# Reordering the hand-over from a network's first layer to its second in a two-layer scan-and-experts kernel

## Time and profile before

| | us |
|---|---|
| median of three runs | 1706.99 |
| lowest and highest run | 1702.88, 1707.31 |
| the profiled execution | 1704.18 |
| its span, first to last instruction | 1702.4 |
| PE busy | 1401.7 (82%) |
| DVE busy | 1130.0 (66%) |
| ACT busy | 736.2 (43%) |
| POOL busy | 570.4 (34%) |

### The profile page before, as it was taken

One profiled execution on the slowest core, in us unless ns is written; L12 is line 12 of the kernel. 1 busy time (PEld: TensorE's weight loads), 2 busy tenths in 40 slices (PEclk: granted clock), 3 DMA queues, 4 the chain that ended last, 5 costly groups with the idle time before them and its releaser, 6 DMA issues.

```text
span 1702.4 us, 23957 instructions
## 1 busy us (share of the span) xinstructions
PE 1401.7 (82%) x8273; PEld 857.9 (50%) x8273; DVE 1130.0 (66%) x2014; ACT 736.2 (43%) x1296; POOL 570.4 (34%) x442
## 2 busy tenths in 40 slices
PE   0156665788887468988979999999999999999998
PEld 0033333344444145655645566666666666666664
DVE  8999967898989546667665555555555555555332
ACT  3465562344444243333214544444444444444332
POOL 1243320132332243132113344344444444444333
PEclk9987776999999778988989999999999999999999
DMA  3434352433332364333126766766676666666454
GB/s 97 150 105 128 106 196 62 141 118 102 123 106 87 133 192 156 136 93 131 45 80 171 189 175 180 181 168 173 180 180 172 172 177 181 178 167 162 89 90 63
DMA packets 91060, 235.58 MB, mean 138 GB/s; under 512 B 13568, under 2 KB 13696, under 8 KB 90944
## 3 DMA queue, kind: packets, MB, share of 16 engines
q1 hardware_dynamic: 56592, 146.20, 25.4%
q0 software_dynamic: 34352, 87.84, 25.0%
HBM read 167.87 MB, written 66.13 MB: 137 GB/s over the span
## 4 chain that ended last, share of the span: by engine, by line
PE 60%; DVE 28%; issue 4%; DMA 3%; ACT 3%; POOL 1%; SPq 0%; POOLq 0%; DVEq 0%; ACTq 0%
PE psG L1442 32%; PE psO L1471 19%; DVE wkFD L1026 6%; PE psH L1451 3%; PE psX L1401 3%; DMA ST<-W 3%; DVE wkFD L1004 2%; DVE wkFN L997 2%; DVE wkFD L993 2%; DVE wkEU L1017 1%; DVE wkFD L1014 1%; DVE wkFN L1033 1%; DVE wkFN L1007 1%; DVE HS L1268 1%; DVE H L1260 1%
## 5 line engine op out<-in xcount | busy, mean ns | idle before, releaser
L1442 PE MATMUL psG<-Whi,XSp 128*128 128x352 f16 (+2 forms) x3000 | 671.2, 329 | 1.7 <-POOL Wlo L715 1.1
L1471 PE MATMUL psO<-Whi,HS 128*128 128x512 f16 (+1 forms) x1180 | 407.5, 398 | 0.0
L1442 PEld LDWEIGHTS psG<-Whi,XSp 128*128 128x128 f16 x3000 | 299.0, 100 | 181.8 <-issue 17.4
L1442 PE MATMUL psG<-Wlo,XSp 128*128 128x352 f16 (+2 forms) x1500 | 388.5, 329 | 0.0
L754 POOL DMA_INDIRECT out<-OB,posb x128 | 201.5, 1574 | 441.9 <-ACT OB L932 441.9
L1236 DVE SCALAR_TENSOR_TENSOR Wlo<-ST,Whi 128x1088 f16<-128x1088 f32 (+1 forms) x122 | 157.2, 1289 | 234.0 <-ACT Whi L892 233.9
L1471 PE MATMUL psO<-Wlo,HS 128*128 128x512 f16 (+1 forms) x590 | 235.6, 399 | 0.0
L912 ACT ACTIVATE H<-psG 128x352 f32<-128x352 f32 (+1 forms) x215 | 95.5, 444 | 259.9 <-PE psG L1442 259.7
L1260 DVE SCALAR_TENSOR_TENSOR H<-H,psG 128x352 f32<-128x352 f32 (+1 forms) x215 | 105.5, 491 | 145.0 <-ACT H L912 144.7
L1442 PEld LDWEIGHTS psG<-Wlo,XSp 128*128 128x128 f16 x1500 | 149.6, 100 | 93.1 <-issue 7.5
L1471 PEld LDWEIGHTS psO<-Whi,HS 128*128 128x128 f16 x1180 | 120.2, 102 | 125.3 <-issue 20.0
(11 more groups left out here) (185 smaller groups left out, 1566.3 us busy)
## 6 DMA issues: line engine op xcount, KB each, us to landing
ST<-W SPq DMA_DIRECT2D x136, 544.0 KB, 4.6
ST<-W SPq DMA_DIRECT2D x27, 512.0 KB, 4.2
slots<-OB SPq DMA_DIRECT2D x39, 256.0 KB, 2.0
wkK<-fT SPq DMA_DIRECT2D x32, 256.0 KB, 3.3
xrows<-XR SPq DMA_DIRECT2D x22, 256.0 KB, 3.7
OB<-x SPq DMA_DIRECT2D x16, 256.0 KB, 3.7
y0rows<-OB SPq DMA_DIRECT2D x16, 256.0 KB, 2.2
out<-OB SPq DMA_DIRECT2D x16, 256.0 KB, 2.1
```

What stands on the lines that cost most here:

```text
L1442: op = M.matmul(o, hx[:, x, q * P:q * P + P], w(half_, off + c, nn), start=first, stop=last)
L1471: op = M.matmul(psO[bank(o)][:, :], HS[a][:, x, q * P:q * P + P], columns[n](half_, off0 + q * 512, 512), start=(q == 0 and x == 0 and hal ...
```

## The change: what it does, and the diff

It has seven parts.

1. `gate_step(i)` is `i + 5`. Steps run to 15 only. What steps 16 to 18 did, and the routing, is now a list written by hand: gates and squares of tiles 11 to 15 first, then turns, logits and shared blocks 9 to 12 between one another.
2. In every odd step from 5 on another piece of weights is split, with a load before and after. Piece 19 is done at the end of step 15 (before: piece 14).
3. Turned tiles 11, 13 and 15 use PSUM bank `psX`, the other tiles of layer 0 `psG[0][1]`; odd tiles use a second buffer for `HT32`; the split forms of tiles 14 and 15 lie in `RT[1]`.
4. The one-hot rows of layer 0 are four wide instructions for 8 rows of 128 (`hot0`), and two for all 32 rows of 39 (in `places0`), where there were 8 times five (`hots`).
5. The counts come with `r_pos` 3, in the same PSUM bank; the copy of positions (`r_posb`) stands apart from `r_wts`.
6. Halves of layer-1 units stand wherever `(j + 5) * 4 // 5` steps up: from j = -3 to 35, one iteration in five without (j = 1, 6, 11, ... 31), and none after 35.
7. `after_half`, which issues the exponentials of the next unit, runs in all iterations.

```diff
 def gate_step(i):
-    return min(i + 5, 17)
+    return i + 5
...
-    for s in range(19):
+    for s in range(16):
...
+        yield from loads(2, 27)
+        if s >= 5 and s % 2 == 1:
+            yield from splits(1)
             yield from loads(2, 27)
-        if s < 3 or s >= 15:
-            yield from splits(2 if s >= 15 else 1)
-        elif s >= 4:
+        if s < 3:
+            yield from splits(1)
+        elif 4 <= s < 15:
             yield from splits(1, low=False)
...
+    def piece():
+        yield from loads(2, 27)
+        yield from splits(1)
+        yield from loads(2, 27)
...
+    yield "f_scale", 10
+    yield "x_load", 15
+    yield "k_turn", 15
+    yield from tiles(("f_tanh",), 14, 15)
+    yield from tiles(("gate", "f_sq"), 11)
+    yield "row", 10
+    yield "gu_pe", 9
+    yield "f_turn", 10
+    yield from tiles(("gate", "f_sq"), 12, 13)
+    yield "f_var", 11
+    yield from tiles(("gate", "f_sq"), 14, 15)
+    yield from tiles(("f_var",), 12, 13)
+    yield "f_scale", 11
+    yield "row", 11
+    yield from tiles(("f_lo", "logit"), 10)
+    yield "f_turn", 11
+    yield from tiles(("f_var",), 14, 15)
+    yield "gu", 9
...
+    yield from tiles(("f_lo", "logit"), 12)
+    yield "f_turn", 14
+    yield from piece()
+    yield from tiles(("f_lo", "logit"), 13)
+    yield "f_turn", 15
+    yield "gu", 10
...
+    yield "gu_pe", 11
+    yield "r_pos", 3
+    yield "r_posb", 3
+    yield from piece()
+    yield "places0", 0
+    for h in range(4):
+        yield "hot0", h
+    yield "h_turn", 10
+    yield "down", 9
     yield "gu_pe", 12
-    yield "r_pos", 3
-    yield "r_wts", 3
-    yield from loads(2, 27)
+    for h in range(4):
+        yield "hot0_pe", h
     yield "table0", 0
     for j in range(3):
         yield "gather", R0 + j
+    yield "gu", 11
+    yield "x2_load", 10
+    yield from piece()
+    yield "r_wts", 3
     for j in range(-4, NB0 + 2):
...
-        if j >= -2 and ((j + 2) * 32 // 42 != (j + 1) * 32 // 42 or j >= 39):
+        if (j + 5) * 4 // 5 != (j + 4) * 4 // 5 or j >= 38:
             yield from next_half()
         if n < S1:
             yield "gu", n
-        if n > R0 - 2:
-            yield from after_half()
+        yield from after_half()
...
-        f_bank = [psG[0][1], psX]
+        def f_bank(f):
+            return psX if f >= NT or f in (11, 13, 15) else psG[0][1]
...
+                after(V.tensor_tensor(B0, bc(iota16[:, 0:NB0].unsqueeze(1), [P, 32, NB0]),
+                                      bc(gj[:, ks].unsqueeze(2), [P, 32, NB0]), ALU.is_equal))
+                b = B0.rearrange("p (i k) n -> p i k n", k=2)
+                after(V.tensor_tensor(b, b, bc(tid.unsqueeze(2).unsqueeze(3), [P, 16, 2, NB0]), ALU.mult))
+
+            def hot0(h):
+                V.tensor_tensor(A0[:, 8 * h:8 * h + 8, :], bc(iota16[:, :].unsqueeze(1), [P, 8, P]),
+                                bc(qa[:, 8 * h:8 * h + 8].unsqueeze(2), [P, 8, P]), ALU.is_equal).then_inc(r_hot, 1)
...
             def f_turn(f):
...
-                if f >= 1:
+                if f == 11:
+                    eng.wait_ge(k_rt, KX)
+                elif 12 <= f < NT:
+                    eng.wait_ge(f_lo, f - 1)
+                elif f >= 1:
                     eng.wait_ge(f_lo, f)
```

More of the change, by code:

```diff
@@ L230, in stages @@
             yield "f_var", i
-        if s < 16:
+        if s < 15:
             yield "k_out", s
@@ L246, in stages, with tiles @@
             yield "dummies", 0
+    def piece():
+        yield from loads(2, 27)
+        yield from splits(1)
+        yield from loads(2, 27)
+    def tiles(what, *which):
+        for i in which:
+            for w in what:
+                yield w, i
+    yield "f_scale", 10
[16 more added lines that the diff above has]
+    yield "gu", 9
+    yield "x2_load", 8
+    yield "h_turn", 8
+    yield from tiles(("f_lo", "logit"), 11)
+    yield from tiles(("f_scale", "row"), 12, 13)
+    yield "down", 7
+    yield from tiles(("f_turn",), 12, 13)
+    yield "r_top", 2
+    yield "r_red", 2
+    yield from tiles(("f_scale", "row"), 14, 15)
+    yield "gu_pe", 10
+    yield from tiles(("f_lo", "logit"), 12)
[4 more added lines that the diff above has]
+    yield "gu", 10
+    yield "x2_load", 9
+    yield "h_turn", 9
+    yield from tiles(("f_lo", "logit"), 14, 15)
+    yield "r_pos", 2
+    yield "r_posb", 2
+    yield "r_wts", 2
+    yield "down", 8
     yield "r_top", 3
     yield "r_red", 3
+    yield "gu_pe", 11
[7 more added lines that the diff above has]
+    yield "down", 9
     yield "gu_pe", 12
-    yield "r_pos", 3
-    yield "r_wts", 3
-    yield from loads(2, 27)
+    for h in range(4):
+        yield "hot0_pe", h
     yield "table0", 0
@@ L475, in pair, with xs, HT @@
             return ap.rearrange("p (a r n) -> p a r n", a=2, r=4)
-        AB = [[pair(RT[1][:, i, :].bitcast(F16)) for i in range(2)],
-              [pair(W[:, 26112:27136]) for W in (Whi, Wlo)]]
+        A0 = RT[0][:, :, :].rearrange("p q n -> p (q n)").bitcast(F16).rearrange("p (r n) -> p r n", r=32)
+        B0 = RT[1][:, :, :].rearrange("p q n -> p (q n)").bitcast(F16)[:, 0:32 * NB0].rearrange("p (r n) -> p r n", r=32)
+        AB = [pair(W[:, 26112:27136]) for W in (Whi, Wlo)]
         idt = OT[:, 0:128]
+        def xs(z):
+            if z in (14, 15):
+                return RT[1][:, z - 12, :].bitcast(F16).rearrange("p (x n) -> p x n", x=2)
+            return XSp[z % 4][:, :, :]
+        def HT(f):
+            return OT[:, 0:512] if f < NT and f % 2 else HT32[:, :]
         idx = [sb("idx0", [P, 39], U32), posb[:, :].bitcast(U32)]
```

142 lines of the change are left out of this document (70 added, 72 removed).

## The result

The median is 1711.08 us (1703.74 to 1712.28 in 12 runs) against 1704.55 (1698.21 to 1707.31 in 12 runs). The ratio is **1.0038, with a 95% interval of 1.0023 to 1.0052: slower, by some 6.5 us.** The profiled executions took 1711.95 (span 1710.1) and 1704.18 (span 1702.4), 7.8 apart; the last output of layer 0's blocks comes at 587.00 instead of 579.12, 7.9 later, and from there to the end it is 1123.1 instead of 1123.3. So the whole loss is made in layer 0.

A forecast was written before the change was run, and what follows sets the result against it. DVE's work was taken as the bound in the steps, only its idle time winnable. Steps +9.1, +6.4, -1.7, hand-over -9.2, units -4.5 and -1.0, end +10.8, -0.4, rounded to +10, gave 1714.5 us; range 1696 to 1722.

The forecast's parts named there:

- Stalls, +9.1: Steps 5, 7 and 11: ACT's gain waits behind a cast whose load is late, costing 3.8, 3.6 and 1.7 us.
- Rival (b): Steps 5, 7 and 11: the second cast finds its load landed, no stall, 9.1 go: 1705 us; chance 0.16.
- Strict order on ScalarE: Steps: ScalarE's queue is strict FIFO, so the gain cannot pass the waiting cast; otherwise the time is 9.1 lower.
- Work moved, +6.4: Steps: low halves of pieces 14 to 18 on DVE now precede unit 15's product, about +6.4 us.
- Hand-over, 48 of work and 29 idle: Unit 15's product to first layer-1 scan: DVE works 48 us, idles about 29; 77.3 against 86.2, scan at 314.5.
- Rival (a): Hand-over: DVE idles 12 us instead of 29, giving 1697.5 us; decided by idle under 13; chance 0.20.
- (d): Hand-over: the two banks do nothing; same time as the forecast, and counted with it in its chance of 0.52.
- First unit, 8.5: First layer-1 scan to first reciprocal: 8.5 us instead of 13.04, so -4.5, reciprocal at 323.0.
- Fifteen periods, 246.9: First to last layer-1 reciprocal: 15 periods of 14.34 plus seven empty iterations at 4.55, 246.9 us against 247.9.
- End, 19.3: Last reciprocal to layer 0's last output: three blocks run uncovered, 19.3 us against 8.5, so +10.8.
- Sum: Layer 0's blocks end at 589.2, 10.1 us later; with -0.4 behind them, all terms rounded to +10.
- Rival (c): Stalls also at steps 9 and 13, PE at half clock through the hand-over, +8: 1722 us; chance 0.12.

The follow-up runs named there:

- the run with two of them: The changed kernel with the extra pieces in odd steps and the new places of the layer-1 halves both undone; 1.0005 against the kernel before.
- the last experiment: The changed kernel with one piece per step, tile 15 loaded in step 15, leftover pieces spread singly through the hand-over; 1694.74 us, 0.9943 against the kernel before.

## Why the prediction was right, and where its terms were off

The forecast of 1714.5 (slower, chance 0.64) against a median of 1711.08: the direction was right, the loss was put at 10 and is 6.5 [3.9 to 8.9 by the interval of the ratio] in the timing and 7.8 in the profile. Point by point:

- **Stalls, +9.1.** The two large ones came within 0.2 where they were put: the period of step 5 grew by 3.76 (forecast 3.8), that of step 7 by 3.45 (3.6), and steps 9 and 13 had none. Rival (b) falls. The step that failed in the mechanism is that only ACT's queue was in it: with the order on ACT mended, 1.9 remained in each, GpSimd's hold on the scan, for which the forecast had no term. At step 11 the queue on ACT was there as forecast and would have cost about 1.5 (1.7), but it was covered by the scan of 172.10, and the 1.85 that was lost is the hold. The term as a whole came out at 9.06 (3.76, 3.45 and 1.85); that the last stands so near its 1.7 is luck.
- **Strict order on ScalarE.** The gain at 87.03 ran behind a cast that had waited 7.51 us for its load, so the rule that the forecast took from the Trainium skill holds in this trace.
- **Work moved, +6.4.** This term was too small. All five low halves did come ahead of unit 15's product, but they took 1.1, 2.3, 1.3, 1.1 and 2.3 from start to start, 8.3 in all: two of them stood beside GpSimd's products and took 2.42 instead of 1.41. The step that failed is "three cost 1.4 and two 1.2", durations from places where GpSimd was quiet. Steps' end 238.87 for 237.2: +1.7, most of it this.
- **Hand-over, 48 of work and 29 idle.** Measured 47.3 and 27.9, first layer-1 scan 314.06 for 314.5. The waits that were named are in the list: tile 15 4.4 (3.7), gate-up 9 3.0 (2.7), gate-up 10 2.6 (2). The middle piece waits 2.4 (2 to 4), the last ones 4.1 and 1.6 (7.5). The one-hot rows took 7.6 (7.2). Rival (a), with an idle time under 13, is refuted, and so is (d), by the run with one bank: the same sum of idle time hides a gain of 5.1 by the banks, used up by the waits that came in place of the old ones. The forecast had both in one number and gave (d) the same time, so the time alone could not have told them apart.
- **First unit, 8.5.** 8.42; the reciprocal at 322.48 for 323.0.
- **Fifteen periods, 246.9.** 243.1. The step "seven at 4.55" was mis-sized: measured 4.4, 4.7, 3.1, 4.7, 4.2, 3.1, 3.1, together 27.3 instead of 31.9; the first and the last period, which are not 14.34, put 0.7 back on. The forecast took 4.55 for the price of an empty iteration between units. The rows make it the price at a mean granted clock of 0.91 (all four such periods of the kernel before stood there); at 1.00 it is 3.1.
- **End, 19.3.** 21.46. The way to the next hidden turn was as told (571.0, 5.5 after the reciprocal), but PE then ran some three microseconds at half clock, which the sum did not have. The five executions without such a spell take 19.8, so the sum itself was 0.5 short.
- **Sum.** The blocks' end at 587.0 for 589.2: steps +1.7, hand-over -2.1, first unit -0.1, units -3.8, end +2.2. Errors of up to 3.8 cancel in it; that the total is 2.2 off is better than its terms. From layer 0's end to the kernel's end the forecast had -0.4, and it is -0.2, no more than such stages differ between runs (1116 to 1128 in these profiles). Rival (c) put more stalls on steps 9 and 13, and none came there; it also had PE's clock low in the hand-over, and that was so (0.67, before 0.72), yet the hand-over was not longer than forecast.
- **Slips in the arithmetic.** Three low halves at 1.4 and two at 1.2 are 6.6, not 6.4; the lower bound of the idle time, 7.5 and half of 3.7 and 2.7, is 10.7, not 12; 86.2 - 77.3 is 8.9, not 9.2; and the terms add up to 9.5 before rounding. None of them moves the forecast by more than 0.5.

By parts, at the blocks' end with the spell taken off, and each as one edit: the extra pieces cost 6.1, the new places of the halves 1.9; the two banks bring 5.4 (5.1 at the first scan), the wide one-hot rows 3.7 (4.1). These do not add up exactly, as the run with two of them shows. What the change loses in the steps is that a step has no idle time on VectorE to put a piece into the earlier trace rows, while the hand-over has 28 us of it.

## What to carry to other kernels

Work moved out of a stretch full of waits into one where the same engine never waits is paid in full, and its transfers, casts and the other engine's share come on top: move it to where the engine idles, and spread it at the pace of the buffers that feed it, as the last experiment did (its gain from the spreading alone is an estimate). When the work of one engine covers another's, finishing the cover early only uncovers what was under it; read the stage behind it before counting the gain. Take a duration from a row in which the same neighbour is at work, not from a quiet one. And before a difference of one or two microseconds is put down to an edit, look whether both executions had the same clock in that stretch.

## What the runs showed of the hardware beyond the forecast

**VectorE and GpSimd held one another.** A forward scan with two operands took 1.20 to 1.22 us alone and 3.07 to 3.08 when a GpSimd low half (128x1024) had begun before it or ran beside it, and that low half 2.63 instead of 2.12 in the case at 81.69; two low halves on VectorE took 2.42 instead of 1.41 beside GpSimd's products, and these 1.61 and 1.71 instead of 1.27. At 181.38 it was GpSimd that lost: its product took 2.09 beside a low half of VectorE that kept its 1.22. The reciprocal, which reads one operand, kept its 3.35 beside the same products. With those GpSimd operations moved away all scans of the stretch were at their 1.2 again. The kernel before shows it twice in the steps, and it could have been read there: the product with two operands at 79.41 took 1.78 instead of 0.75, beside the low half of 78.52, and the one at 92.35 took 1.32. The Trainium skill ("SBUF — State Buffer", the section on the two separate sides) describes the port that the two engines share as an exclusive lock, held for a whole instruction; by that rule the scan of 1.2 at 172.10, behind an operation that has 2.0 to go, takes 3.2, and the trace has 3.07.

**PE's clock behind the same work.** In the end behind the last reciprocal the changed kernel's PE ran at 0.42 per 512-row matmul until about 574.5 and at 0.21 from then on; in five executions with the same records of PE from 2.2 us before the last reciprocal to 5.5 behind it, it ran at 0.21 throughout. That is 21.5 us against 19.8. The two prices of an empty iteration go with the clock in the same way: in the 35 periods with one between units in five traces (the changed kernel, the casts later, one piece per step, tile 15 earlier, the even pieces), each at a mean granted clock of 1.00 took 17.4 to 17.5 and each at 0.91 took 18.5 to 19.1. What decides which of the two an execution gets was not tried.
